# Four transformer layers on one core: rows scaled by GpSimd, means folded into weights, turned context input, early keys of layer 3

## The reference, cut to what matters

```python
x = x + L0_xattn(_layernorm(x), ctx)   # 16 heads; softmax over the QUERIES (axis=1)
x = x + L0_ffn(_layernorm(x))          # switch-head attention: 8 heads of 64, 5 experts for v and o, 2 chosen
x = x + L1_xattn(_layernorm(x), ctx)   # 1 head, only the 32 largest of 77 scores
x = x + L1_ffn(_layernorm(x))          # h = n + gqa(rmsnorm(n)) causal, 16 heads; h + moe(rmsnorm(h)), 8 experts, 2 chosen
x = x + L2_xattn(_layernorm(x), ctx)   # softmax(n @ ctx.T) @ ctx, no weights
x = x + L2_ffn(_layernorm(x))          # quantised: scale from max|x| over ALL rows, silu(gate) * up, quantised again
x = x + L3_xattn(_layernorm(x), ctx)   # 16 heads, causal
x = x + L3_ffn(_layernorm(x))          # relu MLP of width 512
```

## Time and profile before

| | |
|---|---|
| median of 3 runs | 1619.88 us |
| the profiled execution | 1624.02 us |
| its span, first to last instruction | 1622.1 us |
| TensorE busy | 1231.1 us, 76% |
| VectorE busy | 1072.0 us, 66% |
| ScalarE busy | 989.0 us, 61% |
| GpSimd busy | 758.4 us, 47% |
| mean granted clock of TensorE | 0.821 |
| moved by DMA | 18.26 MB, a mean of 11 GB/s |

### The profile page before, as it was taken

The page is one execution under the profiler, slowest core; times in us unless marked ns, Lnnn a source line. Parts: engine busy times, 40 slices in busy tenths (PEclk is TensorE's granted clock), DMA queues, the critical chain, the costliest instruction groups (busy, mean ns, idle before and its releaser), DMA issues. The chain is left out here.

```text
span 1622.1 us, 36294 instructions
## 1 busy us (share of the span) xinstructions
PE 1231.1 (76%) x13755; PEld 920.0 (57%) x13755; DVE 1072.0 (66%) x2499; ACT 989.0 (61%) x3185; POOL 758.4 (47%) x859
## 2 busy tenths in 40 slices
PE   2677877888787897888888898676752558999986
PEld 2566765675664575566666576454431136777764
DVE  3456665788786677886569777755534879855642
ACT  2677778675768778768768866643432334445531
POOL 2038386485882268458245748732110013433431
PEclk9577677889977897997797988688865569999997
DMA  5000000000000000000000000000001100000000
GB/s 143 1 6 1 1 1 1 2 2 1 4 13 1 16 2 2 6 12 1 1 16 2 1 12 1 1 12 1 1 7 48 47 9 7 12 16 9 9 9 14
DMA packets 29637, 18.26 MB, mean 11 GB/s; under 512 B 6456, under 2 KB 27032, under 8 KB 29464
## 3 DMA queue, kind: packets, MB, share of 16 engines
q1 hardware_dynamic: 29464, 15.93, 3.5%
HBM read 11.73 MB, written 4.19 MB: 10 GB/s over the span
## 5 line engine op out<-in xcount | busy, mean ns | idle before, releaser
L1448 DVE TENSOR_REDUCE arena<-pair 128x8 f32<-128x1024 f32 (+2 forms) x224 | 239.7, 1095 | 115.5 <-PE pair L465 49.5
L1019 ACT ACTIVATE arena<-bank 128x512 f32<-128x512 f32 (+5 forms) x352 | 182.0, 540 | 187.1 <-PE bank L417 86.4
L2073 POOL TENSOR_SCALAR_AFFINE_SELECT arena<-arena 128x1024 f32<-128x1024 f32 (+1 forms) x128 | 145.0, 1154 | 287.8 <-ACT arena L1417 145.7
L2111 POOL TENSOR_TENSOR arena<-arena 128x512 f32<-128x512 f32 x160 | 181.3, 1133 | 50.7 <-DVE arena L1565 35.5
L1079 ACT ACTIVATE arena<-pair,arena 77x128 f32<-77x128 f32 x512 | 178.6, 374 | 23.3 <-DVE arena L1448 22.2
L1027 ACT ACTIVATE arena<-arena 128x128 f32<-128x128 f32 x288 | 117.5, 489 | 105.5 <-POOL arena L2084 97.2
L2116 POOL TENSOR_TENSOR arena<-arena 128x512 f32<-128x512 f32 x128 | 175.1, 1368 | 10.0
L417 PE MATMUL bank<-ident,arena 128*128 128x128 f32 (+2 forms) x448 | 85.6, 327 | 120.0 <-ACT arena L1027 62.5
L417 PEld LDWEIGHTS bank<-ident,arena 128*128 128x128 f32 (+2 forms) x448 | 59.2, 171 | 147.4 <-ACT arena L1027 75.1
L2081 POOL TENSOR_SCALAR arena<-arena 128x4 f32<-128x4 f32 x56 | 18.3, 327 | 225.7 <-DVE arena L1455 223.7
L1417 ACT ACTIVATE arena<-pair 77x1024 f32<-77x1024 f32 x64 | 61.8, 1015 | 99.3 <-PE pair L948 99.3
(11 more groups left out here) (255 smaller groups left out, 3001.9 us busy)
## 6 DMA issues: line engine op xcount, KB each, us to landing
arena<-in_ctx SPq DMA_DIRECT2D x24, 154.0 KB
arena<-in_x SPq DMA_DIRECT2D x8, 256.0 KB, 4.6
spill<-arena SPq DMA_DIRECT2D x8, 256.0 KB, 2.1
arena<-spill SPq DMA_DIRECT2D x8, 256.0 KB, 3.7
out<-arena SPq DMA_DIRECT2D x8, 256.0 KB, 2.5
wexp<-in_L_ffn_expert_w SPq DMA_DIRECT2D x1, 512.0 KB, 4.1
arena<-in_L_ffn_w SPq DMA_DIRECT2D x2, 256.0 KB, 3.1
wsq<-in_L_ffn_Wq SPq DMA_DIRECT2D x1, 256.0 KB, 3.1
```

Source lines behind the costliest of these rows:

```text
L1019: return act.activation(dst, src, func, bias=bias, scale=scale)
L1448: return dve.tensor_reduce(dst, src, X, op, **kw)
L2073: return pool.affine_select(out=e, in_=e, compare_op=ALU.is_ge, fill=0.0, base=0, pattern=[[0, 8], [1, 128]], channel_multiplier=-1)
L2111: pool.tensor_tensor(into, xvs[:, b, ex * SHD:(ex + 1) * SHD].unsqueeze(1).broadcast_to([128, SH, SHD]), gates[g % 2][:, b, 0:SH, ex].unsq ...
```

## The change

- Rows scaled by GpSimd. For `n0`, `nf`, `n1`, `ng` and the experts' `nm`, GpSimd multiplies the rows by 1/deviation itself (`scaled`, one 128x512 product) and gives them to TensorE; ScalarE's `apply_norm` stays for `hres`, `n2` and layer 3.
- Means folded into centred weights. Those rows are no longer shifted by their mean. The weights that read them are multiplied once by `centre` (identity minus 1/128), eight products on TensorE with eight copies on ScalarE (`CENTRED`), for layer 1's second block with the norm's weights on it (`centre_w`). The double norm's chain on GpSimd takes both powers in one instruction (`rstd2`).
- Layer 2 scores raw rows against a centred context (`ctxC`); 1/deviation comes in as the scale of the exponential, straight from PSUM. Layer 1's scale 1/sqrt(128) moves into the copy of q; its first top-8 pass and its exponential read PSUM.
- The context also comes turned as an input of its own (`ctx_turned`); the transposes and copies in A and C go.
- Layer 3's keys and values (`kv3`, letter y) are made in the end of A and kept in SBUF; in C ScalarE and VectorE read them from there.
- Experts on two engines: ScalarE's share of layer 0's gated product goes to VectorE (`DVE_OUT = (2, 3, 4)`). x leaves the experts' sum of layer 1 and is added by an instruction of its own.
- `quant2` of stage B and the clearing of C's tiles move from VectorE to GpSimd, which also makes a reduction of other data ahead of the one needed. The output is written from x in place.
- All order strings are new.

```diff
-POOL_OUT, ACT_OUT = (0, 1), (4,)
-DVE_OUT = (2, 3)
+POOL_OUT, DVE_OUT = (0, 1), (2, 3, 4)
...
     ("A", "tensor"):
-        "aaaiaaiibbwabwwcbwbcbbcbacaacaabbbdddddeeceeebffbeeecbbffgeeecbaffhehgcffcaaaabhbhgbcbbhdhgddddeeceh"
...
+        "wiawwwwiwawawabbwbwbwwcbbcbbcaacacabdbbddddecbbeecebeffbeeebcffaaeegceaacffehbhfbgbbfcbhchbdgddbdbdc"
...
+        "iifnnifhnhngjnjnjjnkhnhlkigllikmnhlhlkmilliyyyilmyyyyyymyyimyiyiynynnyjjjjknnklnnlnnlkmnlnklmnlnlmnl"
+        "nmmnnnnnnnnnnnnnnnnn",
...
+        CENTRED = [("x0", w0q, 128), ("f0", wsv[:], NV + 2 * NGATE), ("f0", wsq[:], SH * SHD), ("f0", wsk[:], SH * SHD),
+                   ("x1", w1q[:], 128), ("f1", wgq[:], 128), ("f1", wgk[:], 128), ("f1", wgv[:], 32)]
...
             def weights(g):
                 if g:
                     return
+                for i, (name, w, m) in enumerate(CENTRED):
+                    yield
+                    if name == "f1":
+                        pe.wait_ge(centre_ready, 1)
+                    else:
+                        pe.wait_ge(loaded[name], NLOAD[name])
+                    o = E.take("centred", i)
+                    pe.wait_ge(o.drained, o.n)
+                    mm(o.bank[:, 0:m], (centre_w if name == "f1" else centre)[:], w, start=True, stop=True).then_inc(o.full, 1)
...
+            def kv3(g):
+                yield
+                if g == 0:
+                    pe.wait_ge(loaded["kv"], NLOAD["kv"])
+                mine = ctxT3[:, g * SEQS * CTX:(g + 1) * SEQS * CTX]
+                o = E.take("kv", g, "k")
+                pe.wait_ge(o.drained, o.n)
+                mm(o.bank[:, 0:SEQS * CTX], w3k[:], mine, start=True, stop=True).then_inc(o.full, 1)
+                yield
+                o = E.take("kv", g, "v")
+                pe.wait_ge(o.drained, o.n)
+                for b in range(SEQS):
+                    ins = mm(o.bank[0:CTX, tokens(b)], mine[:, b * CTX:(b + 1) * CTX], w3v[:], start=True, stop=True)
+                ins.then_inc(o.full, 1)
...
+            def scaled(ln, dst, src):
+
+                return pool.tensor_tensor(dst, src, ln.rstd.unsqueeze(2).broadcast_to([128, SEQS, CH]), ALU.mult)
...
             def x0p(g):
                 yield
-                norm(ln0, LN_EPS)
+                spread(ln0, LN_EPS).then_inc(C.give(pool_step), 1)
+                pool.wait_ge(pool_step, C.last(pool_step))
+                if g:
+                    n = E["x0", g - 1, "n"]
+                    pool.wait_ge(n.full, n.n)
+                scaled(ln0, n0, xg[g]).then_inc(C.give(ln0.n), 1)
...
-                tt(y4[g % 2], by_seq(o.bank), x, ALU.add).then_inc(o.drained, 1)
+                tt(x, by_seq(o.bank), x, ALU.add).then_inc(o.drained, 1)
...
-                    reduce(x[:, b, :], moe, ALU.add).then_inc(C.give(m_used), 1)
+                    reduce(nm[:, b, :], moe, ALU.add).then_inc(C.give(m_used), 1)
...
+                tt(x, x, nm, ALU.add).then_inc(C.give(m_x), 1)
...
             pool.drain().then_inc(a_done, 1)
+            pool.partition_all_reduce(gmax[:, 3:4], hmax[:, 0:1], 128, bass.bass_isa.ReduceOp.max)
             pool.wait_ge(amax_ready, 1)
             pool.partition_all_reduce(gmax[:, 1:2], gmax[:, 0:1], 128, bass.bass_isa.ReduceOp.max).then_inc(gmax_ready, 1)
+            pool.wait_ge(a_done, 4)
+            pool.wait_ge(ainv_ready, 1)
...
+                pool.tensor_scalar(qwork, xn[g % 3], ainv[:, 0:1], ROUND, ALU.mult, ALU.add).then_inc(C.give(pool_step), 1)
+                pool.wait_ge(pool_step, C.last(pool_step))
+                pool.tensor_scalar(qwork, qwork, ROUND + QMAX, ROUND - QMAX - 1.0, ALU.min, ALU.max).then_inc(C.give(pool_step), 1)
+                pool.wait_ge(pool_step, C.last(pool_step))
+                pool.tensor_scalar(xqs[g % 2], qwork, ROUND, None, ALU.subtract).then_inc(C.give(b_q), 1)
+
+            merge(ORDER["B", "gpsimd"], {"a": quant2})
+            for each in vdiag3:
+                pool.memset(each, 0.0)
+            pool.memset(nm3, 0.0)
+            pool.drain().then_inc(c_zeroed, 1)
...
+                if g == 5:
+                    o = E["x0", NG - 1, "o"]
+                    sp.wait_ge(o.drained, o.n + 1)
+                    for dst, src in LOADS["kv"]:
+                        sp.dma_start(dst, src).then_inc(loaded["kv"], 16)
```

473 lines of the change are left out of this document (226 added, 247 removed).

## The result

The changed kernel takes 1607.2 us (median of 19 runs, 1593.1 to 1617.7) where the kernel before takes 1619.9 on the same chip (19 runs): a ratio of 0.991, 95% interval 0.9886 to 0.9934. The ratio is taken over fast runs alone, without the changed kernel's slowest run, 1617.7 us, which counts as slow; the two medians give 0.992. The forecast was 1558: the direction came true, the size did not, 13 us instead of 62.

A forecast was written before the change was run, and what follows sets the result against it. It took A as bound by waits between engines, B by VectorE, C by TensorE (VectorE at entry). Terms +9 -4 -45 -6 +4 +0 -5.6 -14 = -62 from 1624.0, less 4.1, gave 1558 us; range 1505 to 1615.

The forecast's parts named there:

- Stage A, forecast -42 in all (+9 -4 -45 -6 +4): Stage A in us: start +9, rest of ramp -4, steady part -45, last group's end -6, layer 3's keys and values +4.
- The weighting of the relief: A's steady part: 35% of the 77 us of ScalarE-released waits outside row scaling go, 27 us.
- the steady part's 45 us: A from 155 to 1090 us: 43 us of TensorE's waits go, taken as 45 with the clock.
- One of its signs of being wrong: Stage A: the forecast is wrong if GpSimd's waits become the releaser of TensorE's transposes; no size given.
- The start: Start of A: new TensorE order delays first scores from 35.35 to 44 to 46 us, +9 (bounds +5, +12).
- Relief without effect: Rival, A: ScalarE's waits pass to VectorE, steady part gives 5 instead of 45 us; 1598 us, chance 0.20.
- GpSimd's queue: Rival, A: 40 scaled writes each delay masks and products queued behind on GpSimd, +85 us; 1643 us, chance 0.08.
- The lock: Rival, A: scaled writes and VectorE hold each other up over SBUF, +36 to +52 us; 1602 us, chance 0.05.
- Seam, forecast 0 (-1 to +3): A to B: clearing and early reduction don't shorten the path, rows land later; up to +3 for GpSimd's second switch.
- B, forecast -5.6: Stage B: VectorE loses three passes a group, third product starts earlier, beat 5.90 to 5.2 us; 0.7 times 8.
- C, forecast -14: Stage C: TensorE loses 2.2 us a group; 11 us gained where full, 3 at entry, none at end (-8 to -20).
- Where it is full (five groups) this is all gain: Stage C, five groups with TensorE 94% busy: the 2.2 us a group removed count fully, 11 us.

The follow-up runs named there:

- a_load: Changed kernel with 256 tiny useless copies added on ScalarE in layer 0's feed-forward; 1624.1 us, 1.003 of the kernel before.
- before_one_copy: Kernel before, with ScalarE making one 128x512 product for expert 4 instead of eight 128x64 products; 1610.2 us, 0.990 of the kernel before.
- two_hybrid: Changed kernel, C in old order with useless TensorE work replacing the removed except v's passes, B's first two quantisations on VectorE; 1581.1 us, 0.977.
- b_vector: Changed kernel with B's quantisation and the clearing of C's tiles back on VectorE, no early GpSimd reduction; 1594.4 us, 0.985 of the kernel before.
- c_slots: Changed kernel, C in old order, useless TensorE work exactly where the removed work stood; 1580.2 us, 0.978 of the kernel before.
- c_slots_tiny: As c_slots, but each useless piece is only two products of one column, same turn of the banks; 1594.8 us, 0.986 of the kernel before.
- c_order: Changed kernel with stage C in the order of the kernel before, the removed work still out; 1590.9 us, 0.983 of the kernel before.

## Why the prediction was wrong, point by point

- **Stage A, forecast -42 in all (+9 -4 -45 -6 +4): the size held, in part by luck.** Measured about -46. The weighting of the relief (a third of it on the path) is what a_load and before_one_copy found. But the prediction booked 43 of the steady part's 45 us as waits of TensorE that go, and TensorE to be over 84% busy; its idle time fell by 14 us only and it stayed at 81%. The other part is shorter busy time, with fewer instructions and at a higher clock, for which the prediction had 2 us. One of its signs of being wrong came true: GpSimd's waits became a releaser of TensorE's transposes (L2064, 9.9 us). The start was priced too high: the first scores came at 39.6 to 42.1, not 44 to 46; in the changed kernel's profile the centring products took 1.02 us a 512-wide pair, where 1.4 and up to twice that were booked. "Relief without effect" and "GpSimd's queue" (85 us) fell; GpSimd's queue is real, 24 us of waits, and already inside the 46. The lock is small in sum, if these rows are the lock's: GpSimd's 160 and 128 products became 26 and 45 ns longer in the mean (1133 to 1159, 1368 to 1413), 10 us of its busy time, and VectorE's new addition of x, booked at 0.68 us, took 1.20 in the median of eight (0.68 to 1.52). VectorE's work in A grew by 24 us where 15 were booked.
- **Seam, forecast 0 (-1 to +3): the step failed, +6.3.** It named the second switch and capped it at 3 us with no row for it; GpSimd's first pass began 8.6 us behind its reduction. Of the 6.3 us, 4.3 are this later start (12.7 us behind A's end instead of 8.4). The other 2.0 are the slower passes: 3.4 us from the first one's start to B's first product instead of 1.5, which the prediction saw in part (2 against 1.4) and booked at nothing. A bound without a row should have been taken from the nearest one, the 5.75 us of the first switch. It also said that neither clearing nor an early reduction could shorten the path, since the rows' landing is the later. In the kernel before, VectorE was at work without a gap from its second clearing to the first quantisation at 1251.90, and the rows, landing from 1251.1 on, were not the last. two_hybrid's 7.6 us agree: without the clearing the first quantisation began 2.6 us earlier behind A's end than in b_vector, and it did not wait for the rows, which were fetched from 3.0 us behind A's end on in both.
- **B, forecast -5.6: mechanism right, size 0.7 of it.** The beat went from 5.90 to 5.31 us (1217.06 to 1222.37) with VectorE idle 1.3 us before each third product, as predicted: 0.6 a group instead of 0.7, and the stretch gave 3.9. GpSimd's passes take 2.8 us together, under the beat. Clearing on GpSimd cost C nothing in the old order (329.5 with it, 329.6 without).
- **C, forecast -14: the step that sank the forecast, +19 to +29.** "Where it is full (five groups) this is all gain" took TensorE's 94% busy as work that sets the end. Part of it was work that covered waits which stayed, and the missing activity cost the clock. This is 10 us more than before instead of 14 less, by c_slots against c_slots_tiny. The other 9 to 19 us are the new order of C, by c_order against the changed kernel. The prediction read "all order strings are new" and priced C by its work alone, as if an order were neutral. What in the new order does it was not taken apart; its first 100 us have the clock at 0.65 and TensorE's instructions down to 887 from 1234.

The forecast used the clock for A, where it did rise (0.83 to 0.86), and took C's 1.00 for granted. That 1.00 hung on the work that the change took away.

## What to carry to other kernels

Before you book work taken from a nearly full TensorE as time, look for the next wait in its queue, also some steps behind: up to the length that the wait can grow, the work is free already, and its going can cost the clock of the passes behind it. Price a new order of work as an edit of its own, and test it by running the new code in the old order. A load that moves to GpSimd right behind one of its reductions starts late, here by 8.6 us, besides the 5.9 us ahead of the reduction; give the first steps to another engine.

## What the runs showed of the hardware that was not expected

- Useless passes of TensorE at the right places made C 10 us shorter (329.6 to 319.4), with the granted clock rising from 0.75 to 0.87 in its first 100 us and from 0.96 to 1.00 in its steady part; behind a wait of 1.5 us instead of 0.6 the same 32 passes took 2.0 us instead of 1.1. The same amount in one place cost 10 us in the old order (339.2 against 329.5); in the new one C took 350.1, with 338.0 to 348.2 without it.
- GpSimd took 8.6 us from its reduction to its next standard instruction in the changed kernel, and 7.6 to 9.3 in the ten profiles with this sequence; on the way in it took 5.9.
- GpSimd's 128x512 pass with one input takes 0.61 to 0.69 us, and 1.49 us when it writes bf16; its power over 128x8 took 1.67 us where 128x4 takes 1.08, so that taking two together saves less than half.
- Stage A's length varied by 24 us between executions of the same code, its steady clock between 0.83 and 0.86; before and after differ by twice that.
